# Two attention units whose softmax sums come from ScalarE's row passes instead of matmuls with ones

## The reference

```python
scores = einsum('bnqd,bnkd->bnqk', q, k) * HEAD_DIM ** -0.5
scores = where(causal, -inf, scores)
attn = softmax(scores, axis=-1)      # exp(s - max) / sum(exp(s - max)) over keys
out = einsum('bnqk,bnkd->bnqd', attn, v)
x = x + out.transpose(...).reshape(B, S, H) @ W_out.T + b_out
```

## Time and profile before

| | us |
|---|---|
| median of 3 runs | 2078.03 |
| the profiled execution | 2077.43 |
| its span in the trace | 2075.7 |
| TensorE busy | 2031.5 |
| VectorE busy | 1188.5 |
| GpSimd busy | 1000.2 |
| ScalarE busy | 688.7 |

### The profile page before, as it was taken

One profiled execution on the slowest core, in us unless ns is written; L12 is line 12 of the kernel. 1 busy time (PEld: TensorE's weight loads), 2 busy tenths in 40 slices (PEclk: granted clock), 3 DMA queues, 4 the chain that ended last, 5 costly groups with the idle time before them and its releaser, 6 DMA issues.

```text
span 2075.7 us, 34948 instructions
## 1 busy us (share of the span) xinstructions
PE 2031.5 (98%) x10816; PEld 1445.1 (70%) x10816; DVE 1188.5 (57%) x2451; ACT 688.7 (33%) x1222; POOL 1000.2 (48%) x775
## 2 busy tenths in 40 slices
PE   7999999999999999999999999999999999999998
PEld 5555588888755558888775555888887555588887
DVE  4766554445676655454457665545456767544554
ACT  2344432221144452222114445222221444432221
POOL 4224259763312436975331243697533223379743
PEclk9999999999999999999999999999999999999999
DMA  5333101111333311111243331111113333111112
GB/s 153 88 87 73 32 31 61 52 61 42 83 73 83 73 33 40 61 51 51 72 134 73 83 73 35 38 61 51 51 42 83 73 83 73 42 41 61 51 51 81
DMA packets 59177, 134.11 MB, mean 65 GB/s; under 512 B 10720, under 2 KB 11744, under 8 KB 58976
## 3 DMA queue, kind: packets, MB, share of 16 engines
q1 hardware_dynamic: 58976, 131.66, 22.4%
HBM read 76.57 MB, written 4.19 MB: 39 GB/s over the span
## 4 chain that ended last, share of the span: by engine, by line
PE 92%; issue 3%; DVE 3%; ACT 1%; DMA 1%; POOL 0%; DVEq 0%; SPq 0%; POOLq 0%; ACTq 0%
PE bank L1364 13%; PE bank L1236 11%; PE bank L1238 11%; PE bank L1237 11%; PE ring L1236 10%; PE ring L1237 9%; PE ring L1238 9%; PE ring L1314 9%; PE bank L1342 7%; PE ring L1227 1%; DVE xn L979 1%; DMA x<-x_in 1%; ACT prob L782 0%; DVE stats L919 0%; DMA out<-x 0%
## 5 line engine op out<-in xcount | busy, mean ns | idle before, releaser
L979 DVE CUSTOM_DVE_ANT_0 xn<-ring,mask_row 128x128 bf16<-128x128 f32 (+7 forms) x512 | 372.2, 748 | 110.0 <-PE ring L1314 106.1
L661 POOL TENSOR_SCALAR_AFFINE_SELECT prob<-prob 128x512 f32<-128x512 f32 x128 | 82.3, 643 | 524.1 <-ACT prob L782 414.1
L782 ACT ACTIVATE prob<-bank 128x512 f32<-128x512 f32 (+1 forms) x512 | 264.5, 570 | 211.8 <-PE bank L1342 211.0
L584 POOL TENSOR_SCALAR area<-w_stage 128x1024 fp32r<-128x1024 f32 x129 | 139.8, 1084 | 377.5 <-PE bank L1238 206.3
L586 POOL TENSOR_TENSOR area<-w_stage,area 128x1024 fp32r<-128x1024 f32 x129 | 309.1, 2396 | 10.8
L1038 DVE TENSOR_TENSOR x<-x,bank 128x512 f32<-128x512 f32 x256 | 170.9, 685 | 233.2 <-PE bank L1238 233.2
L1236 PE MATMUL ring<-xt_hi,area 128*128 128x512 f32 x672 | 265.9, 396 | 1.9 <-DVE area L1071 1.3
L1237 PE MATMUL ring<-xt_lo,area 128*128 128x512 f32 x672 | 263.2, 392 | 0.0
L1238 PE MATMUL ring<-xt_hi,area 128*128 128x512 f32 x672 | 262.9, 391 | 0.0
L1314 PE MATMUL ring<-area 96*128 96x512 f32 (+3 forms) x768 | 239.1, 373 | 6.7 <-DVE row_max L979 5.5
L1314 PEld LDWEIGHTS ring<-area 96*128 96x128 f32 x768 | 130.2, 188 | 160.5 <-DVE row_max L979 117.8
(11 more groups left out here) (153 smaller groups left out, 3320.4 us busy)
## 6 DMA issues: line engine op xcount, KB each, us to landing
w_stage<-ffn_w SPq DMA_DIRECT2D x96, 512.0 KB, 3.3
area<-kq_parts SPq DMA_DIRECT2D x336, 128.0 KB, 2.3
w_stage<-attn_w SPq DMA_DIRECT2D x35, 512.0 KB, 3.3
area<-attn SPq DMA_DIRECT2D x48, 128.0 KB, 2.3
x<-x_in SPq DMA_DIRECT2D x20, 256.0 KB, 3.7
out<-x SPq DMA_DIRECT2D x16, 256.0 KB, 2.5
bias_rows<-row_bias SPq DMA_DIRECT2D x10, 256.0 KB, 4.0
area<-nm_hi SPq DMA_DIRECT2D x32, 8.0 KB, 1.8
```

The source lines that it names most:

```text
L584: pool.tensor_scalar(hi, src, 1.0, 0.0, ALU.mult, ALU.add).then_inc(w_hi_done, 1)
L782: act.activation(prob[:, step % 2, h, off:], scores_at(u, j, h), ACT.Exp, scale=SCALE).then_inc(prob_ready, 1)
L979: dve.tensor_tensor_reduce(out=sum_out[:, RING[name] % 2, 0:keys], in0=src[:, 0:keys], in1=mask_row[:, TOKENS - keys:], scale=1.0, scalar= ...
```

## The change

Units 3 and 5 become "summed" units. Their row tiles are written negated, masked and scaled to `masked` (three f32 buffers in SBUF) while VectorE takes the minimum of each row. ScalarE then makes one pass over each of these tiles: exp with the row's minimum as bias, in place, with the sum of the row as a second output (`row_sums`). After the 16th it takes the logarithm of the sums and an exp of its negative (`row_logs`). VectorE multiplies that inverse by the sum and uses the result as a first-order correction (`shift`): what is transposed and stacked is the maximum plus the logarithm of the sum. The exps of the transposed tiles are then the finished probabilities. In these units "sums" matmuls, the copy of `den_bank`, the reciprocals and the normalisation are left out.

With it go: EARLY from 12 to 9 for units 3 and 5 (three row tiles of each are made one unit later); new POINTS for units 1 to 5; the second q/k part on VectorE two items later (LO_BEFORE); the last `weigh` ahead of the transpose in summed units; steps of summed units in the order heads 0 and 1, values, head 2, head 3; and a table set for ScalarE that is loaded by name.

```diff
-EARLY = {1: 2, 3: 12, 5: 12, 7: 12}
+EARLY = {1: 2, 3: 9, 5: 9, 7: 12}
...
-LO_BEFORE = {0: (2, 5), 1: (2, 5), 3: (2, 5), 5: (2, 5)}
-STEP_PARTS = (((0,), ("values",), (1,), ("sums",)), ((0,), (1,), ("values", "sums"), ()))
+LO_BEFORE = {0: (2, 5), 1: (2, 7), 3: (2, 7), 5: (2, 7)}
+STEP_PARTS = (((0,), ("values",), (1,), ("sums",)), ((0,), (1,), ("values", "sums"), ()),
+              (("head 0", "head 1"), ("values",), ("head 2",), ("head 3",)))
...
+    (("project", 0, range(0, 2)),
+     ("last",),
+     ("max",),
+     ("project", 0, range(2, 4)),
+     ("s1", 2),
+     ("project", 1, range(0, 2)),
+     ("s1", 1),
+     ("scores", 0, 1),
...
+SUMMED = (3, 5)
+MASKED_BUFS = 3
+EXP_TABLE = "natural_log_exp_and_others"
...
+                def row_sums(u, t):
+
+                    act.wait_ge(ring_drained, drained(it, ("s1", u, t)))
+                    k = tile_index(u, t)
+                    tile = masked[:, k % MASKED_BUFS, 0:(CT + t % CT + 1) * P]
+                    act.activation(tile, tile, ACT.Exp, bias=row_max[:, u % 2, t:t + 1], scale=-1.0,
+                                   accum_out=row_sum[:, t:t + 1]).then_inc(row_summed, 1)
+
+                def row_logs(u):
+
+                    n = it * UNITS + (SUMMED.index(u) + 1) * SHIFT
+                    act.wait_ge(row_summed, it * SUM_TILES + tile_index(u, GH * CT - 1) + 1 + MASKED_BUFS)
+                    act.activation(row_log[:, :], row_sum[:, :], ACT.Ln).then_inc(log_done, SHIFT)
+                    act.wait_ge(log_done, n)
+                    act.activation(row_inv[:, :], row_log[:, :], ACT.Exp, scale=-1.0).then_inc(inverse_done, SHIFT)
+
+                def row_sums_beside(u, slot):
+
+                    early = sum(BETWEEN.get(u, ()))
+                    for (what, *which), at in zip(beside(u)[early:], points(u)):
+                        if what == "s1" and which[0] in SUMMED and at // 2 + 1 == slot:
+                            row_sums(*which)
+                            if which[1] == GH * CT - 1:
+                                row_logs(which[0])
...
                     for j in range(1, key_tiles(u)):
-                        exps(u, j, range(GH))
+                        exps(u, j, range(GH // 2))
+                        if not narrow(u, j):
+                            row_sums_beside(u, 2 * (j - 1))
+                        exps(u, j, range(GH // 2, GH))
+                        if narrow(u, j):
+                            row_sums_beside(u, 2 * (j - 1))
+                        row_sums_beside(u, 2 * (j - 1) + 1)
...
-                load_table(ACT.Exp)
+                act.preload_act_table_set(EXP_TABLE)
...
+                    if u in SUMMED:
+                        k = tile_index(u, s)
+                        wait_alone(dve, row_summed, it * SUM_TILES + k + 1)
+                        dve.tensor_tensor_reduce(
+                            out=masked[:, k % MASKED_BUFS, 0:keys], in0=src[:, 0:keys],
+                            in1=mask_row[:, TOKENS - keys:], scale=-SCALE, scalar=3.3e38, op0=ALU.add, op1=ALU.min,
+                            accum_out=row_max[:, u % 2, s:s + 1]).then_inc(ring_drained, 1)
+                        return
...
+                def shift(u):
+
+                    n = it * UNITS + (SUMMED.index(u) + 1) * SHIFT
+                    least = row_max[:, u % 2, :]
+                    dve.wait_ge(inverse_done, n)
+                    dve.tensor_tensor(row_inv[:, :], row_inv[:, :], row_sum[:, :], ALU.mult)
+                    dve.tensor_tensor(row_log[:, :], least, row_log[:, :], ALU.subtract).then_inc(shift_step, SHIFT)
+                    dve.wait_ge(shift_step, n)
+                    dve.scalar_tensor_tensor(least, row_log[:, :], 1.0, row_inv[:, :], ALU.add, ALU.subtract
+                                             ).then_inc(shift_ready, SHIFT)
...
+                    if u in SUMMED and what == "sums":
+                        return
```

More of the change, by code:

```diff
@@ L201 @@
      ("op", 1, range(2, 3)),
-     ("scores", 2, 3)))
+     ("scores", 2, 3)),
+    (("project", 0, range(0, 2)),
[6 more added lines that the diff above has]
+     ("scores", 0, 1),
+     ("project", 1, range(2, 3)),
+     ("s1", 2),
+     ("scores", 2, 3),
+     ("project", 1, range(3, 4)),
+     ("s1", 1)))
 LAST_FILL = ((6, "op", 0, range(3, 4)),
@@ L225, with since_last, tile_index @@
 STACKED = ((0, 2), (0, 3), (1, 2))
+SUMMED = (3, 5)
+MASKED_BUFS = 3
+EXP_TABLE = "natural_log_exp_and_others"
+def since_last(u):
+    return 2 if u - 1 in SUMMED else 1
+SHIFT = UNITS // len(SUMMED)
+def tile_index(u, s):
+    return SUMMED.index(u) * GH * CT + s
+SUM_TILES = len(SUMMED) * GH * CT
 def block_kernel(nc, x_in, attn_w, ffn_w, qk_bias, row_bias, out):
@@ L262, in block_kernel @@
         w_stage = sb("w_stage", [P, 2, SLOT])
+        masked = sb("masked", [P, MASKED_BUFS, TOKENS])
+        row_sum = sb("row_sum", [P, GH * CT])
+        row_log = sb("row_log", [P, GH * CT])
+        row_inv = sb("row_inv", [P, GH * CT])
         table_out = sb("table_out", [1, 1])
@@ L1126, in iteration @@
                 for u in range(-1, UNITS - 1):
-                    parts = list(range(RECIPS)) if u > 0 else []
+                    parts = list(range(RECIPS)) if u > 0 and u - 1 not in SUMMED else []
                     def some_recips(count):
@@ L1358, in weigh @@
                         if j == 0 and u:
-                            pe.wait_ge(evacuated, it * UNITS + u)
+                            if u - 1 in SUMMED:
+                                pe.wait_ge(attn_ready, it * UNITS + u)
+                            else:
+                                pe.wait_ge(evacuated, it * UNITS + u)
+                    if u in SUMMED and what == "sums":
+                        return
                     for h in range(GH):
@@ L1365, in weigh @@
                                         stop=j == key_tiles(u) - 1, tile_position=(0, h * HEAD))
-                    if what == "sums":
+                    if what == "sums" or u in SUMMED:
                         ins.then_inc(pv_done, 1)
@@ L1539, in between @@
                         early += count
-                    for what, *which in UNIT_START[max(unit(u)[1], u - UNITS + 4)]:
+                    for what, *which in UNIT_START[4 if u in SUMMED else max(unit(u)[1], u - UNITS + 4)]:
                         if what == "project":
@@ L1556, in iteration @@
                     for j in range(1, key_tiles(u)):
-                        for part in STEP_PARTS[narrow(u, j)]:
+                        for part in STEP_PARTS[1 if narrow(u, j) else 2 if u in SUMMED else 0]:
                             for what in part:
@@ L1561, in iteration @@
                                     scores_t(u, j, 2 * what + 1)
+                                elif what in HEAD_BY_HEAD:
+                                    scores_t(u, j, HEAD_BY_HEAD.index(what))
                                 else:
```

30 lines of the change are left out of this document (22 added, 8 removed).

## The result

The kernel after took 2080.62 us (median of 22 runs, 2078.61 to 2082.74), the kernel before beside it 2077.56 (22 runs). The ratio is 1.0016, 95% interval [1.0010, 1.0022]. The forecast was 2050 (2032 to 2066), and it gave "no change" 5%. The profiled execution has a span of 2080.1 us. First line: engines as in the earlier trace rows; then TensorE's waits, which answer to the earlier trace rows. TensorE's largest item of waiting, 14.4 us in 2 waits for the LayerNorm's `xn`, lies outside these units and stands in neither list; its total is the same before and after.

A forecast was written before the change was run, and what follows sets the result against it. The prediction took TensorE as the bound, busy 2031.5 of 2075.7 us. Removed matmuls save 50.8 us and new waiting costs 23, so 28 us less: 2050 us, range 2032 to 2066 for 8 in 10.

The forecast's parts named there:

- sums leave TensorE: Units 3 and 5: removing the `ones` matmuls saves 6.35 us a unit, 50.8 us over four passes.
- waits on VectorE and ScalarE beneath: Units 3 and 5: new TensorE waiting for VectorE, 1.7 us in unit 5 and 1.0 in unit 3 a pass.
- tiles change place: Three score tiles each of units 3 and 5 move one unit later; nothing is added on TensorE.
- chain of the maximum, stack, units 2 and 4: Per pass: 1.6 us chain and 0.1 stack for each of two summed units, plus 0.2 for unit 4's delayed exps.
- unit 6: Unit 6's values wait for one copy instead of two, a gain of 0.5 us a pass.
- VectorE in units 3 and 5: TensorE stalls for VectorE to empty ring buffers: 1.3 and 0.4 us in unit 5, 1.0 in unit 3.
- The shift's steps at 0.1 each: Three small VectorE instructions before the transpose of the maxima take 0.1 us each, with a wait between.
- tables stay: ScalarE's table loads stay two a pass; the rival that Ln and Exp reload tables, 2071 us, had 3%.
- ScalarE over 85% in unit 3: Sign expected in the trace after: ScalarE busy over 85% of unit 3.
- TensorE's busy time down by 51 us: Sign expected in the trace after: TensorE's busy time falls by near 51 us with the removed matmuls.
- slower: Rival: ScalarE becomes the bound at 1.5 us a row pass, 62 us of waiting against 50.8 saved: 2089 us; 8%.
- more waiting: Rival: 1.2 us row passes and three `masked` buffers slowing VectorE, 42 us of waiting: 2069 (2062 to 2074); 17%.

The follow-up runs named there:

- h5: e7 with the full-width exps of units 3 and 5 cut to 128 columns; 2016.0 us, ratio 0.9710 to the kernel before.
- e2: The kernel before without the `ones` matmuls in units 3 and 5, nothing else of the change; 2055.9 us, ratio 0.9889.
- e7: e2 with reciprocals over 4 of 64 columns and row maxima over 128 keys of each row tile in all units; 2027.76 us, ratio 0.9764.
- h4: The kernel before with only the change's new EARLY, POINTS (unit 7's kept) and LO_BEFORE, sums kept as matmuls; 2084.42 us, ratio 1.0041.
- e4: The kernel after with GpSimd's split of weights in unit 3 moved behind its first mask; 2066.5 us, ratio 0.9945 to the kernel before.
- g4: e4 with reciprocals from point 2, a third score bank, EARLY 12 for units 3 and 5 and POINTS to fit; 2062.46 us, ratio 0.9929.
- f4: e4 with the idle `den_bank` as third buffer for the scores of summed units; 2065.99 us, ratio 0.9954 to the kernel before.
- h2: e4 with e7's short VectorE work and a third score bank in summed units; 2040.84 us, ratio 0.9825 to the kernel before.
- g5: e4 with reciprocals from point 2, a third score bank, EARLY 11 for units 3 and 5 and POINTS to fit; 2061.4 us, ratio 0.9930.

## Why the prediction was wrong, step by step

In units 1 to 6 the forecast was -12.7 + 5.8 = -6.9 us a pass; the table of units gives +1.1, and the measured terms add up to +1.0. The terms are of the second pass. Over all four, the last but one is 2.6 instead of 3.0.

| step, us a pass | forecast | measured | by |
|---|---|---|---|
| sums leave TensorE | -12.7 | -12.7 (with both covers gone -13.0) | h5 |
| waits on VectorE and ScalarE beneath | +2.7 | +7.0 | e2, e7, h5 |
| tiles change place | 0 | +2.0 | h4 |
| chain of the maximum, stack, units 2 and 4 | +3.6 | +1.7 | e4 less e2 and h4 |
| late VectorE instruction and clock | in the chain at 0.1 | +3.0 | e4 |
| unit 6 | -0.5 | (-0.35, within the first and the fourth row) | table of units |

**The step that failed** is "VectorE in units 3 and 5": 1.3 + 0.4 us in unit 5 and 1.0 in unit 3, 2.7 in all, where e2 lost 7.0. I placed most of the waiting at the first wide tile, and took the rest of the 12.7 us as gain because TensorE had hardly waited before. But the 5.5 us of the earlier trace rows were low because the `ones` group between two row tiles was just the time in which VectorE emptied a buffer. e2 shows 4 to 5 more waits a summed unit, none over 0.6 us, and unit times of 32.6 and 31.95 us where 6.35 less would be 29.0 and 28.1. What I did not do was lay all 23 tiles of the shortened unit against their buffers. Of the 7.0 us, short VectorE work brings back 4.2. The other 2.8 are waiting for the exps that free the score banks (short exps on top bring 3.1), for which the forecast had no term in units 3 and 5, and which no ScalarE share of 47% shows.

**"Score tiles only change place"** was counted at nothing, and is 2.0 (h4). The same matmuls took 0.27 us each in unit 2 and freed 0.205 in unit 1; 0.7 of the 2.0 are waits.

**The chain** was right in its members and too dear: the last values waited 0.4 us at most for GpSimd's mask (forecast 0.7), the transpose 0.92 in unit 5 (forecast 0.9). By the table e4 less e2 is 3.7 us a pass, and 2.0 of them are the order. The 1.7 left is a difference that takes these costs as additive. It also holds the new order of parts within the steps of units 3 and 5, which no run tried by itself. The row passes came out as priced, slightly under:

```profile
L842 ACT ACTIVATE masked<-masked,row_max 128x1024 f32<-128x1024 f32 x32 | 36.7, 1148 | 1.1 <-DVE row_max L1057 1.0
...
L842 ACT ACTIVATE masked<-masked,row_max 128x640 f32<-128x640 f32 x32 | 26.4, 825 | 0.0
L842 ACT ACTIVATION_READ_ACCUMULATOR masked<-masked,row_max 128x1 f32 x128 | 25.0, 195 | 0.0
```

Start to start they take 0.81 (640 columns) and 1.13 (1024), against 0.87 and 1.19.

**The shift's steps at 0.1 each**: two are (646.13 to 646.22), the third took 2.12 where it met GpSimd's subtraction. I had named GpSimd's mask as a neighbour of the chain, not GpSimd's split of weights at the start of unit 3, and no bound of mine covered it. The Trainium skill, "SBUF — State Buffer" (Who interferes with whom), says that a VectorE instruction with two inputs from SBUF contends with a GpSimd instruction that reads SBUF, and that whichever issues second waits for the first; the run agrees, 0.18 us alone and 2.12 to the end of the other. One row does not fit as simply: the second step (646.22) also has both inputs in SBUF and starts 0.01 us after GpSimd's record, in all four passes, and is not held (0.17 us). The traces do not show why.

**Right**: f32 output instead of bf16 costs nothing (`masked` 1223 ns at 1024 columns, `xn` 1219 before); tables stay, nine loads, so that rival falls; the row passes beside unit 1 are nearly hidden (34.3 us against 34.0 in h4, which has the same tiles and no row passes); `ones` records 1024. ScalarE over 85% in unit 3 was wrong, it stands at 69% of a unit that did not get shorter. TensorE's busy time down by 51 us was wrong too (28.9), since the dearer tiles, the matmuls at the lower clock and the hidden waits count as busy. The rival "slower" had the wrong engine, ScalarE at 1.4 us a pass; "more waiting" pointed at the three `masked` buffers, and what VectorE waited there (`masked` on L842) does not stand among TensorE's own waits.

## What to carry to other kernels

A group of matmuls that stands between two uses of a double buffer is also the time in which another engine empties the buffer; before counting its removal at full price, lay the drain times of every tile in the shortened stretch against the new distances, and expect a second engine just below the first. A wait of nearly nothing before says how well the work was balanced, not how much slack there is. A busy share can hide waits between matmuls: compare the length of the same row in two runs. On a serial chain of small instructions, look at what GpSimd runs in just those microseconds, and put large two-input GpSimd work elsewhere: here this was worth 10 us of 2080 in units 3 alone, where the change with it out of the way gains 7.6 in units 1 to 6. And look at the granted clock of every pass before calling two schedules equal.

## What the runs showed of the hardware

- A VectorE instruction on 128x16 with two SBUF inputs takes 0.18 us alone and 2.12 us beside a GpSimd subtraction of 128x1024 (2.38 us), in 4 of its 8 executions, all in unit 3. The normalisation on 128x512 takes 0.69 us, and 1.37 beside a GpSimd subtraction of 128x512 (1.28 us) in e2.
- Behind the TensorE wait of 2.87 us the granted clock was at 1.2 GHz for 3.4 us in three passes of four, and matmuls of 512 columns came every 0.43 us instead of 0.23; behind waits of 0.92 us it stayed at 1.00. In the first unit 3 of g4 the clock was at the lower level for 10 us, behind a stretch whose longest listed wait of TensorE was 0.8 us; the same unit one pass later stayed at 1.00 with the same wait of 0.8. Stretches of 3 to 11 us at the lower clock stand in one unit 5 each of e2, f4 and h2 and in one unit 3 of g5 as well. What set them off is open.
- Reading the accumulator costs ScalarE 0.09 us from start to start though its record is 0.19 us long.
- Ln and Exp of 16 columns take 0.21 and 0.22 us, 0.31 from the start of one to the other with the wait between them, and no table load.
